# Second pass and overflow stage of a four-layer graph kernel: one post fewer per step, indices by half groups, the first overflow block outside its loop

## The reference, cut to what matters

```python
x = _layernorm(x + L0(x, edge_index, edge_type_64))      # mean over incoming edges of (x[src]+rel[type]) @ W.T + b
x = _layernorm(x + L1(x, src, dst, edge_weight))         # attention with 4 heads, softmax over the edges of a row
x = _layernorm(x + L2(x, edge_index, edge_type_2))       # one of two projections by the edge's type, summed
x = _layernorm(x + L3(x, edge_index))                    # sum weighted by 1/sqrt(deg[row]*deg[col]), with self loops
```

## Time and profile before

| | us |
|---|---|
| median of 3 runs | 6277.53 (6276.63 to 6278.22) |
| the profiled execution | 6280.96 |
| its span, first to last instruction | 6279.2 |
| mean granted TensorE clock | 0.949 of full |
| busy: PE | 5405.9 |
| busy: PE weight loads | 4327.7 |
| busy: DVE | 4634.8 |
| busy: ACT | 2130.0 |
| busy: POOL | 1589.7 |

### The profile page before, as it was taken

The page is one execution under the profiler, slowest core; times in us unless marked ns, Lnnn a source line. Parts: engine busy times, 40 slices in busy tenths (PEclk is TensorE's granted clock), DMA queues, the critical chain, the costliest instruction groups (busy, mean ns, idle before and its releaser), DMA issues. The chain is left out here.

```text
span 6279.2 us, 121898 instructions
## 1 busy us (share of the span) xinstructions
PE 5405.9 (86%) x44062; PEld 4327.7 (69%) x44063; DVE 4634.8 (74%) x11931; ACT 2130.0 (34%) x3318; POOL 1589.7 (25%) x1592
## 2 busy tenths in 40 slices
PE   4899999999998118999949999999499999986998
PEld 3777777777776116767649999999377777764666
DVE  7777777778777217788859999999455555556888
ACT  0111111111111004444413333333266666653665
POOL 0577777777777740000000000000000000000000
PEclk9999999999999559999969999999699999997999
DMA  2100000000000000000000000000000000000000
GB/s 77 24 2 2 2 2 2 2 2 2 2 2 2 2 34 4 1 1 2 1 3 1 1 1 1 1 1 1 2 1 1 1 1 1 1 1 2 7 7 10
DMA packets 60230, 33.57 MB, mean 5 GB/s; under 512 B 51583, under 2 KB 54097, under 8 KB 59598
## 3 DMA queue, kind: packets, MB, share of 16 engines
q1 hardware_dynamic: 8622, 22.14, 1.1%
q0 software_dynamic: 50176, 3.31, 0.8%
q10 hardware_dynamic: 1056, 2.86, 0.2%
HBM read 13.67 MB, written 14.54 MB: 4 GB/s over the span
## 5 line engine op out<-in xcount | busy, mean ns | idle before, releaser
L1376 ACT ACTIVATE gC<-qC 128x768 bf16<-128x768 f32 (+3 forms) x1960 | 1611.8, 823 | 1745.4 <-PE qC L1414 1740.2
L1515 PE MATMUL qO<-X,gC 128*128 128x384 bf16 x9604 | 1932.1, 326 | 8.6 <-ACT gC L1376 8.6
L607 POOL DMA_INDIRECT records<-rec,idx x1568 | 1580.6, 1008 | 520.1 <-issue 494.6
L70 DVE TENSOR_TENSOR g<-iota_b,recs 128x768 bf16<-128x768 bf16 (+3 forms) x1970 | 1196.9, 643 | 577.6 <-PE qC L1414 526.8
L1414 PE MATMUL qC<-g 128*128 128x128 bf16 (+1 forms) x12029 | 1204.5, 242 | 100.4 <-DVE g L70 57.4
L1414 PEld LDWEIGHTS qC<-g 128*128 128x128 bf16 (+1 forms) x12029 | 1070.8, 136 | 262.0 <-DVE g L70 68.6
L1515 PEld LDWEIGHTS qO<-X,gC 128*128 128x128 bf16 x9604 | 889.0, 98 | 458.3 <-ACT gC L1376 13.2
L401 DVE SCALAR_TENSOR_TENSOR junk<-pK,key,earlier 128x128 f32<-128x128 f32 (+3 forms) x1568 | 767.9, 546 | 34.8 <-issue 27.0
L511 PE MATMUL pG<-run,hT 49*128 49x98 f32 x3136 | 793.4, 432 | 0.0
L558 ACT ACTIVATE hT<-pT 49x512 f32<-49x512 f32 x393 | 232.1, 591 | 1553.4 <-PE pT L488 1553.4
L511 PEld LDWEIGHTS pG<-run,hT 49*128 49x128 f32 x3136 | 697.2, 324 | 71.0 <-issue 71.0
(11 more groups left out here) (278 smaller groups left out, 4093.0 us busy)
## 6 DMA issues: line engine op xcount, KB each, us to landing
records<-rec,idx POOLq DMA_INDIRECT x1568, 2.1
records<-null SPq DMA_DIRECT2D x31, 256.0 KB, 9.5
recs<-records SPq DMA_DIRECT2D x1, 4866.0 KB, 14.0
B<-in_x SPq DMA_DIRECT2D x1, 2744.0 KB
out<-B SPq DMA_DIRECT2D x7, 392.0 KB
ety<-in_edge_type ACTq DMA_DIRECT2D x2, 686.0 KB
esrc<-in_src SPq DMA_DIRECT2D x1, 686.0 KB
edst<-in_dst SPq DMA_DIRECT2D x1, 686.0 KB
```

The lines of the kernel that those rows point to most:

```text
L70: return v.tensor_tensor(o.rearrange("p n (a b) -> p n a b", b=2), iota_b[:, 0:w].rearrange("p (a b) -> p a b", b=2).unsqueeze(1).broadcas ...
L607: gp.indirect_dma_start(rec_d, bass.IndirectOffsetOnAxis(ap=idx[:, k:k + 1], axis=0), rec[:, k, :], None).then_inc(s_sent[g % 2], 16)
L1376: act.activation(Cs[:, u % 2, 0:n, :], pC[u % 2][:, 0:n, :], ACT.Copy).then_inc(s_cs, 1)
L1515: mm = pe.matmul(pO[i % SUMS][:, 0:width], Cs[:, u % 2, j, :], x, start=first, stop=last)
```

## The change

Second pass:

- Posts. PE no longer posts after the keys (s_krow) and after the add (s_add); one post after the turn (s_turned) remains, and that of the look-up (s_look). DVE's ranks and ACT's copies wait for s_turned. ACT copies run ahead of hT. The buffers of one-hots have no semaphore of their own any more (s_hot_free).
- Indices. `places(g, par, hf)` handles eight columns (HALF): it runs after quad 1 and after quad 3, after quad 1 ahead of `hot`. POOL waits for each eight.

Overflow stage, on DVE, ACT and PE alike: the block of chunks is a function, called once for block 0 and, inside `If(NOB < count)`, in a loop over the other 27. On DVE the one-hots of chunk j + 1 are made before chunk j is added.

```diff
+def places(g, par, hf):
+    h = 2 * g + hf
+    mine = slice(hf * HALF, (hf + 1) * HALF)
+    cols = bass.ds(g * GROUP + hf * HALF, HALF)
+    v.wait_ge(s_base, (h + 1) * (HALF // QUAD) + 2)
+    v.tensor_reduce(base[:, mine, :], prod[:, mine, :, :], AX.X, ALU.add).then_inc(s_pos, 1)
...
+    v.scalar_tensor_tensor(out=idx[:, cols], in0=posl[:, mine], scalar=float(NREC), in1=posh[:, mine],
+                           op0=ALU.mult, op1=ALU.add).then_inc(s_idx, 1)
 def hot(g, par):
-    v.wait_ge(s_hot_free, g + 1)
...
-            v.wait_ge(s_krow, q + 3)
+            v.wait_ge(s_turned, q + 1)
...
+            if w % 2 == 1:
+                places(g, par, w // 2)
             if w == 1:
                 hot(g + 1, 1 - par)
-        v.wait_ge(s_base, (g + 1) * (GROUP // QUAD) + 2)
-        v.tensor_reduce(base[:, :, :], prod[:, :, :, :], AX.X, ALU.add).then_inc(s_pos, 1)
...
 def keys_and_turn(q, w, par, g):
...
-    mm.then_inc(s_krow, 1)
...
-    mm.then_inc(s_tr, 1)
+    mm.then_inc(s_turned, 1)
...
-            mm.then_inc(s_add, 1)
...
-        pe.wait_ge(s_add, (g + 1) * (GROUP // QUAD) + 1)
-        pe.sem_inc(s_hot_free, 1)
...
+                    act.wait_ge(s_turned, q + 1)
                     act.wait_ge(s_look, q + 1)
-                    act.wait_ge(s_add, q + 1)
                     act.activation(run[:, w % 2, 0, :], pR[0:NT, 0:NT], ACT.Copy).then_inc(s_run, 1)
-                    turned(q + 1, w + 1)
+                    act.activation(hT[:, w % 2, :, :].rearrange("p k n -> p (k n)"), pT[w % 2][0:NT, 0:QUAD * P], ACT.Copy).then_inc(s_ht, 1)
...
-for g in range(2 * NG2):
+for g in range(4 * NG2):
     gp.wait_ge(s_idx, g + 1)
-    for k in range(g * GROUP, (g + 1) * GROUP):
+    for k in range(g * HALF, (g + 1) * HALF):
         gp.indirect_dma_start(rec_d, bass.IndirectOffsetOnAxis(ap=idx[:, k:k + 1], axis=0), rec[:, k, :], None).then_inc(s_sent[g % 2], 16)
```

```diff
-with v.Fori(0, NI // NJ) as o:
-    with v.If(o * NOB < count):
-        codes(o)
-        with v.Fori(0, NJ) as j:
...
+def block_of_chunks(o):
+    codes(o)
+    hots(o, 0)
+    with v.Fori(0, NJ - 1) as j:
+        with v.If((o * NJ + j) * (2 * PAIR) < count):
+            with v.If((o * NJ + j + 1) * (2 * PAIR) < count):
+                hots(o, j + 1)
+            add(o, j)
+    with v.If((o * NJ + NJ - 1) * (2 * PAIR) < count):
+        add(o, NJ - 1)
+
+with v.If(0 < count):
+    block_of_chunks(0)
+    with v.If(NOB < count):
+        with v.Fori(1, NI // NJ) as o:
+            with v.If(o * NOB < count):
+                block_of_chunks(o)
```

More of the change, by code:

```diff
@@ L482, in keys_and_turn @@
                                 for part, st in ((ts64_b, True), (td_b, False)):
-                                    mm = pe.matmul(pK[w % 2][:, k * P:(k + 1) * P], part[:, bass.ds(col, 1)].broadcast_to([P, P]), ident_b[:, :], start=st, stop=not st)
-                            mm.then_inc(s_krow, 1)
+                                    pe.matmul(pK[w % 2][:, k * P:(k + 1) * P], part[:, bass.ds(col, 1)].broadcast_to([P, P]), ident_b[:, :], start=st, stop=not st)
                             pe.wait_ge(s_ht, q + 1)
@@ L499, in _ @@
                                     for k in range(QUAD):
[L500 to L501 removed]
+                                        pe.matmul(pR[0:NT, 0:NTE + P], hts[:, par, w * QUAD + k, 0:NT], htd[:, par, w * QUAD + k, :], start=False, stop=False, skip_group_check=True)
                                     if w + 1 < GROUP // QUAD:
@@ new lines, in hots, with add @@
+                        def hots(o, j):
+                            for par in range(2):
+                                hot(2 * (o * NJ + j) + par, j * (2 * PAIR) + par * PAIR, par)
+                        def add(o, j):
+                            for par in range(2):
+                                g = 2 * (o * NJ + j) + par
+                                bs = tiles_of(v, 2 * j + par, by_source)
+                                v.wait_ge(s_o, g + 3)
+                                for k in range(PAIR):
+                                    v.wait_ge(s_acc, (g + 2) * PAIR + k)
+                                    dst = acc[:, bass.ds(bs[k], 1), 0:width].rearrange("p a w -> p (a w)")
+                                    v.tensor_tensor(dst, dst, pO[par][:, k, 0:width], ALU.add).then_inc(s_acc, 1)
@@ L831, in _ @@
                                                 if mode == "relation":
-                                                    pe.matmul(pO[par][:, k, P:P + 1], Cs[:, par, k, P:2 * P], one_b[:, :], start=True, stop=True)
-                                                if mode == "weighted":
-                                                    mm = pe.matmul(o_k, Cs[:, par, k, :], A[:, bass.ds(As[k], 1), :].rearrange("p a w -> p (a w)"), start=True, stop=True)
-                                                else:
@@ L836, in _ @@
                                                     for s in range(3):
-                                                        mm = pe.matmul(o_k, Cs[:, par, k, 0:P], X[:, bass.ds(As[k], 1), s, :].rearrange("p a w -> p (a w)"),
-                                                                       start=(s == 0), stop=(s == 2 and not by_source))
-                                                    if mode == "relation":
-                                                        for s in range(3):
-                                                            mm = pe.matmul(o_k, Cs[:, par, k, P:2 * P], relx[:, s, :], start=False, stop=(s == 2))
@@ L842, in _ @@
-                                                    if mode == "typed":
-                                                        for s in range(3):
-                                                            mm = pe.matmul(o_k, Cs[:, par, k, P:2 * P], X2[:, bass.ds(As[k], 1), s, :].rearrange("p a w -> p (a w)"),
-                                                                           start=False, stop=(s == 2))
-                                            mm.then_inc(s_o, 1)
+                                                        mm = pe.matmul(o_k, Cs[:, par, k, P:2 * P], relx[:, s, :], start=False, stop=(s == 2))
@@ new lines, in block_of_chunks @@
+                                                if mode == "typed":
+                                                    for s in range(3):
+                                                        mm = pe.matmul(o_k, Cs[:, par, k, P:2 * P], X2[:, bass.ds(As[k], 1), s, :].rearrange("p a w -> p (a w)"),
+                                                                       start=False, stop=(s == 2))
+                                        mm.then_inc(s_o, 1)
+                        with pe.If(0 < count):
+                            block_of_chunks(0)
+                            with pe.If(NOB < count):
+                                with pe.Fori(1, NI // NJ) as o:
+                                    with pe.If(o * NOB < count):
+                                        block_of_chunks(o)
```

127 lines of the change are left out of this document (57 added, 70 removed).

## The result

The changed kernel takes 6138.9 us (four runs: 6133.6, 6133.9, 6144.0 and 6144.4) where the kernel before takes 6277.9 in the same measurement. The ratio is 0.9779, with an interval of 0.9766 to 0.9791: 139 us faster, where 110 were forecast. The four runs lie at two levels 10.5 us apart; only one of the lower level, the one at 6133.9, was profiled, and what parts the levels isn't known. That run has a span of 6132.1, that is 147.1 us less than the 6279.2 of before. All that follows accounts for those 147.1, of which the sum had 109.9. Where a later text says "the pass" it is the second pass.

What follows compares the result with a forecast made beforehand. POOL's late start, 1568 scatters and drain were taken to bound the second pass. Empty trips 73.5, early one-hots 27.4 and earlier start 9.0 sum to 109.9 us off 6277.5: 6168 us, range 6152 to 6206.

Steps and rivals of the forecast that it cites:

- What bounds the pass: Second pass: late start, 1568 POOL scatters and drain set its length; after the change POOL still ends last, by 7.6 us.
- From then on POOL is never short if its 21.2 us a group hold: Second pass: after the start, POOL does not run out of indices, with sixteen scatters at 1.324 us each, 21.2 us.
- Start of the scatters, 9.0 us: Second pass: half groups of indices let POOL's first scatter start at 198.94 instead of 208.28 us, gaining 9.0 us.
- The group, 20.61 us: Second pass: sixteen columns take DVE and PE 20.61 us instead of 18.61, so DVE ends at 2278.6 us.
- Rival (a): Second pass: DVE and PE end last if a half index chain exceeds 2.88 us; 6190 at 3.03, 6204 at 3.1; chance 0.20.
- Empty trips, 73.5 us: Overflow stages: one false test replaces 27 empty outer trips, cutting DVE's idle behind the four stages by 73.5 us.
- One-hots ahead, 27.4 us: Overflow stages: building one-hots a chunk ahead removes 33.3 us of PE's waits, less a charge, gaining 27.4; bounds 18 to 33.
- The charge of 5.9 us: Overflow stages: PE cannot start a chunk instantly, so a loop trip of 0.74 us is charged eight times.
- (b): Second pass: a half chain costs 3.68 us like a whole one, POOL starves, 6317 us; decides from 3.48; chance 0.03.
- (c): Overflow stages: jumps over the duplicated block code cost more than the trips saved, 6174 to 6207 us; chance 0.06.
- (d): Overflow stages: early one-hots bring nothing as PE waits as long for DVE's sums, 27.4 us less gain, 6195; chance 0.05.
- Posts at nothing: Second pass: dropping the posts of keys and adds gains nothing; at most 56 us off DVE's end, none off the pass.

Runs made afterwards that it cites:

- peel_only: The kernel before with the first overflow block outside the loop, one-hots still built in each chunk's own trip: 7126.0 against 7199.0 us (0.9888).
- half_over_c: The kernel before with index chains in halves, its old posts, and the change's overflow stages: 6144.1 us where before takes 6283.7 (0.9778).

## Why the prediction was right or wrong

- **What bounds the pass**: right. POOL's start, its scatters and its drain set the end, DVE was meant to come within 8 us, and came 1.7 us past it.
- **"From then on POOL is never short if its 21.2 us a group hold"**: this is the step that failed. POOL was indeed never short (1.9 us of waits behind the first), but the 21.2 did not hold. I took the 1.324 us between scatters as a price of the scatter. It is 1.263 and a loss that depends on where DVE's one-hots begin: 78.9 us in before, 45.7 in the change. With the old pitch POOL would have been through at about my 2286.2 and the pass would have ended there; it ended at 2256.0, 30.2 us earlier. That the pitch isn't a constant could be seen ahead of time: the earlier trace rows give a scatter's median beside a maximum over twice as long, and the change moves the very instructions that stand beside the long ones. I passed over it. Which way it would go could not be read from those rows; that it fell was luck of the phase.
- **Start of the scatters, 9.0 us**: 8.4 (first scatter at 199.92, said 198.94).
- **The group, 20.61 us**: 20.37. The reduce of half a group takes 0.97 us (said 0.99), the half chain 2.57 us ahead of the one-hots and 2.83 ahead of the ranks on average (said 2.88). The 0.24 us, 97 times, put DVE's end at 2256 and not at 2278.6. No run splits them.
- **Rival (a)**, DVE ends last: half of it came true. DVE does end last, but at an end that is 30 us earlier than POOL's of the forecast, so it costs 1.7 us. Its price per half chain was not reached.
- **Empty trips, 73.5 us**: 73.6 in peel_only's trace, and 1.6 more inside the stages. The change itself leaves 13.14 us of idle in place of 86.95, 73.8 less. That it comes so near is in part luck: the same empty trips leave 86.4 to 92.1 us of idle, by the kernel around them.
- **One-hots ahead, 27.4 us**: 31.6, within the bounds of 18 to 33, but not by that sum. The ceiling of 33.3 was right (33.1 by the rows, of which 1.7 are left). The charge of 5.9 us came out larger, not smaller: 5.3 more of "issue" and 3.7 more of waits for DVE's sums. What outweighs it is a term that I had at nothing: PE's matmuls in the stages take 9.7 us less, at a higher granted clock. That the number lies in its bounds is luck to that degree.
- **Rivals (b), (c), (d)**: none came. Half a chain costs less than 3.48; no new stall of 1 us stands at the head of the stages' trips (in the first stage DVE's idle "issue" ahead of a chunk's one-hots is 0.71 us where it was 0.51, and 1.52 at most between two sums where it was 1.12). The Trainium skill (page Runtime: NRT & Kernel Launch, section Instruction fetch mechanics) says that a taken branch whose target lies outside the two pages held waits for a fetch, so the change might have paid there; the idle of 2.8 to 3.7 us behind the stages leaves that no room beyond the 3.35 that I had left for the barrier and the skipped trips. No row shows where a page ends.
- **The clock**, of which (b) says that the trace shows none below 1.00 in this pass: that holds for the stretch of the earlier trace rows only. In before it was 0.81 from 2008 to 2082 us and 0.50 from there to 2295, where PE did nothing; in the change it was 0.85 from 2184 to 2256. Whether it helped to put DVE's end there isn't shown.
- **Posts at nothing**: right for this result as far as is known, since the end of the pass was set to within 1.7 us by POOL; between the traces of the change and half_over_c, where DVE sets it, they show as 0.09 us a group.
- **The range** took in unknowns of the parts I had split out and none of the term that I had held constant, and that was the largest in the pass.

## What to carry to other kernels

When an engine's instruction has a median of 960 ns and a maximum of 2000, its mean is not its price: find what stands beside the long ones and ask whether the change moves that. Two loops that run freely beside each other can stay near the worst phase for a whole pass; a step of a few tenths of a microsecond in one was then worth tens of microseconds here (94.0 against 10.9 us of loss, by 0.15 us), so a gain of that kind is to be tested by a dummy instruction before it is put down to the change. A term that comes out right can hide two that cancel: look at the busy time and the granted clock of a stretch, not only at its waits.

## What was not expected of the hardware

- An indirect DMA issue on POOL that begins inside DVE's 128x2048 one-hot instruction takes 1.97 us in place of 0.96 (the longest in the traces 2.03); one that begins 0.08 us ahead of it takes 0.99. The loss against the phase is a sawtooth from 0 to 1.05 us, the same in all five kernels on three chips.
- A kernel became 24.5 us faster by one more DVE instruction a group (0.9960, 0.9944 to 0.9976), on the one chip of that kind.
- With the one-hots of the overflow stages made ahead, the granted clock in the first stage was 0.86 in place of 0.68, and the same matmuls kept PE busy for 16.8 us in place of 21.2.
- The kernel before took 6278 us where the change was measured, and 6284, 7042, 7199, 7239 and 7252 on the five chips of the experiments; in the traces taken the whole of the difference is in the second pass, where two engines start 8 and 11 us after the matmul that should release them.
- On two of these chips the change is worth 4.5%, on the chip of the forecast 2.2%.
